# Narrow attention: project all heads once, stack rows by one-hot products, contract over 32 rows per head

## The chip, the cores and the metric

The kernel runs on one core of a Trainium2 chip. The metric is the device time of one execution in microseconds (us), lower is better. The profile is one profiled execution on the same core.

## The reference

A stack of four gated blocks works on x of shape (4, 256, 128), that is 1024 tokens of width 128, with a context of the same shape. Each block adds an attention and then a feed-forward layer to the residual. Two of the four attentions are "narrow": 16 heads of width 8. Only these are touched.

```python
# block 0
Q = (query @ Wq.T).reshape(B, T_q, 16, 8)      # query = layernorm(x)
K = (context @ Wk.T).reshape(B, T_c, 16, 8)
V = (context @ Wv.T).reshape(B, T_c, 16, 8)
attn = softmax(einsum('bqhd,bkhd->bhqk', Q, K) / sqrt(8))
out = einsum('bhqk,bkhd->bqhd', attn, V).reshape(B, T_q, D) @ Wo.T
# block 2: the same without any weights: Q = layernorm(x), K = V = context
x = x + tanh(g) * out
```

## The kernel before

Everything stays in SBUF. The narrow attention is `small_pe`, `small_act`, `small_dve`, called with c=0 for block 0 and c=1 for block 2. Heads go in NG = 4 groups of GH = 4; tokens go in two halves of 512 (two batches each). One (group, half) is a slot, x in the code; there are eight slots in each attention, the first four in a hardware loop (`Fori`), the other four written out.

Precision: the products run in fp32r, so each fp32 operand is split into a high part and a low remainder. A head takes a block of 32 rows in the 128 partitions: 24 rows hold three copies of its 8 numbers (high with high, high with low, low with high in one contraction), and rows 24 and 25 carry minus the row maximum.

For each slot, in this kernel:

- `project` (L350) makes q or k of one group and half in three 128x512 products (`mm3`, L180 to L182) in bank 5, from weights in which the columns of each head stand three times. ACT's `high` (L456) copies the bank as the high part, DVE's `stack` (L511) builds the stacked rows from both.
- `masked_keys` (L518, DVE) makes four copies of the stacked keys, each with only one head's 32 rows left. So every product of scores contracts over all 128 rows, though only 32 are non-zero.
- `maxima` (L359, PE) makes the scores with queries as rows, in eight steps of two 256-column products, in turn in banks 6 and 7; `largest` (L524, DVE) takes the row maxima of each step. Step n waits for the reduction of step n-2. This is done for slot x+1 during slot x.
- `minus` (L533, L534) splits the negated maxima, `maxima_back` (L367) transposes them, `queries` (L538) adds them to the stacked queries.
- `scores` (L374) makes transposed scores in four steps of four products; ACT takes the exponential of each step (L471, 128x1024). `values` (L384) multiplies with the values and a column of ones, with the four heads in the four 32-column groups of the output, in four steps. ACT copies the sums (L474), `sums_back` (L392) transposes them, `normalise` (L546, L547) divides.

Each engine works through a queue written out by hand. That of PE in one slot: scores 0, maxima 0 and 1, scores 1, maxima 2 and 3, values 0, scores 2, three products of `project`, maxima 4, values 1, maxima 5, scores 3, maxima 6, values 2, maxima 7, values 3, `sums_back`, `maxima_back`, and `project` of the queries of x+3, which waits for `normalise`. Ahead of slot 0 stands an opening: four times projection, high part and stacked rows, each waiting for the one before (one bank, one tile); masked keys; eight maxima steps; transposes.

Of the kernel before, what the change touches and what calls it, by code (L numbers as in the profile page):

```python
# [51 lines left out]
for _name, _width in (  # L52
    ("ident", P), ("spread", 2 * P), ("den_ones", 5 * BLK), ("lo_q", 1), ("lo_k", 1), ("one_rows", 1), ("head", GH),
    ("inv_n", 2 * NT), ("iota", E), ("gates", 8), ("nbias", 1), ("alpha", 1), ("rb2", E), ("ebias", E),
    ("rb1", 1), ("gamma", E), ("beta", E), ("b1", 4 * E), ("b2", E), ("quant_bias", P),
    ("ln_l_w", 1), ("ln_l_b", 1), ("ln_c_w", 1), ("ln_c_b", 1), ("bo", P),
    ("centroids", E), ("gate_w", E), ("router_w2", E), ("b_experts", P),
    ("W_Q", P), ("W_K", P), ("W_inv", P), ("router_w1", P), ("W_O", P), ("wv0", P), ("wo0", P),
    ("quant_w", P), ("lora_a", P), ("lora_b", P), ("sel_e", E * P),
):  # L60
    SMALL[_name] = (N_SMALL, _width)
    N_SMALL += _width
# [59 lines left out]
def build(nc, x, ctx_tok, ctx_t, mask, small, wa0, wf0, wb1, wf1, wa2, wb3, wf3, out):  # L122
    stack = ExitStack()
    with stack:  # L124
# [32 lines left out]
        RB1, RA2, CAP = 0, NQ * W_B, NQ * W_B + NG * W_A  # L157
# [27 lines left out]
        ld = {n: sem("loaded_" + n) for n in ("x", "ctx_t", "ctx_tok", "small", "mask", "a0", "f0", "b1", "f1", "a2", "b3", "f3")}  # L185
# [124 lines left out]
        A = signals("a", NG, w=2, q=4, hi=4, y=4, km=8, v=2, mx=16, red=16, m2=2, mt=2, yf=2, s=8, p=8, pv=8,  # L310
# [3 lines left out]
        a_y, a_yf, a_ky = wr[:, 0:1024], wr[:, 1024:2048], wr[:, 2048:3072]  # L314
        a_km = [wr[:, 3072 + 1024 * j:4096 + 1024 * j] for j in range(GH)]
        a_hi = wr[:, 7168:8192]
        a_wh, a_wl = wr[:, 8192:8448], wr[:, 8448:8704]
        a_vall = wf[:, 0:1024]
        a_vg = wf[:, 1024:2048].rearrange("p (t j c) -> p t j c", t=NT, j=GH)
        a_p = [wf[:, 2048 + 1024 * k:3072 + 1024 * k] for k in range(2)]  # L320
        a_m2 = wf[:, 4096:5120].rearrange("p (t j c) -> p t j c", t=NT, j=GH)
# [7 lines left out]
        def small_passes(eng, slot):  # L329


            with eng.Fori(0, NG - 2) as i:
                slot(i, 0, True, True, True)
                slot(i, 1, True, True, True)
            slot(NG - 2, 0, True, True, True)
            slot(NG - 2, 1, False, True, True)
            slot(NG - 1, 0, False, False, True)
            slot(NG - 1, 1, False, False, False)

        def small_pe(pe, c, m):  # L340
            def at(i, name, k):
                pe.wait_ge(A[name].sem, A[name].at(c, i, k))

            def project(i, x, k):
                h = x % 2
                at(i, "w", 2 * (x // 2) + 2)
                if k:
                    at(i, "y", 2 * x + 1)
                src = (half(ch, h), half(cl, h)) if k else (half(xh, h), half(xl, h))
                mm3(bank(5), (a_wh[:, k * P:(k + 1) * P], a_wl[:, k * P:(k + 1) * P]), src).then_inc(A["q"].sem, 1)  # L350

            def maxima(i, x, n):
                t, j0 = 4 * (x % 2) + n // 2, 2 * (n % 2)
                if n == 0:
                    at(i, "km", 4 * x + 4)
                if n >= 2:
                    at(i, "red", 8 * x + n - 1)
                for j in range(j0, j0 + 2):
                    last = nc.tensor.matmul(ps[:, 6 + n % 2, (j % 2) * S:(j % 2 + 1) * S],  # L359
                                            a_y[:, t * P:(t + 1) * P], a_km[j][:, (t // 2) * S:(t // 2 + 1) * S],  # L360
                                            start=True, stop=True)
                last.then_inc(A["mx"].sem, 1)

            def maxima_back(i, x):
                at(i, "m2", x + 1)
# [5 lines left out]
            def scores(x, u):  # L371
                b, kb = 2 * (x % 2) + u // 2, u % 2
                for j in range(GH):
                    last = nc.tensor.matmul(ps[:, 2 * (u % 2) + j // 2, (j % 2) * S:(j % 2 + 1) * S],  # L374
                                            a_km[j][:, b * S + kb * P:b * S + (kb + 1) * P],
                                            a_yf[:, b * S:(b + 1) * S], start=True, stop=True)
                last.then_inc(A["s"].sem, 1)

            def values(i, x, u):
                if u == 0:  # L380
                    at(i, "v", x + 1)
                at(i, "p", 4 * x + u + 1)
                for j in range(GH):
                    last = nc.tensor.matmul(ps[BLK * j:BLK * (j + 1), 4, (u // 2) * S:(u // 2 + 1) * S],  # L384
                                            a_vg[:, 4 * (x % 2) + u, j, :], a_p[u % 2][:, j * S:(j + 1) * S],
                                            start=u % 2 == 0, stop=u % 2 == 1)
                last.then_inc(A["pv"].sem, 1)

            def sums_back(i, x):
                at(i, "raw", x + 1)  # L390
# [5 lines left out]
            def slot(i, x, asking, projecting, maxing):  # L396
                def more(*tiles):
                    for n in tiles if maxing else ():
                        maxima(i, x + 1, n)

                at(i, "yf", x + 1)
# [12 lines left out]
                scores(x, 3)  # L414
                more(6)
                values(i, x, 2)
                more(7)
                values(i, x, 3)
                if projecting:
                    at(i, "y", 2 * (x + 2) + 2)  # L420
                sums_back(i, x)
                if maxing:
                    maxima_back(i, x + 1)
                if asking:
                    at(i, "att", x + 1)
                    project(i, x + 3, 0)

            for x in range(2):
                pe.wait_ge(s_xs, 2 * splits(m) + x + 1)
                if x:  # L430
                    at(0, "y", 2)
                project(0, x, 0)
                project(0, x, 1)
            for n in range(8):
                maxima(0, 0, n)
            maxima_back(0, 0)
            at(0, "y", 4)
            project(0, 2, 0)
            small_passes(pe, slot)

        def small_act(act, c):
# [7 lines left out]
            def at(i, name, k):  # L449
                act.wait_ge(A[name].sem, A[name].at(c, i, k))  # L450

            def high(i, x, k, used=True):
                at(i, "q", 2 * x + k + 1)
                if used:
                    at(i, "y", 2 * (x - 1) + k + 1)
                nc.scalar.activation(half(a_hi, k), bank(5), ACT.Copy).then_inc(A["hi"].sem, 1)  # L456

            def value_tiles(i, x):
                t = slice(4 * (x % 2), 4 * (x % 2) + 4)
                nc.scalar.activation(a_vg[:, t, :, 0:DH8],  # L460
                                     vsrc[:, t, bass.ds((i + x // 2) * BLK, BLK)].rearrange("p t (j d) -> p t j d", j=GH),
                                     ACT.Copy).then_inc(A["v"].sem, 1)

            def slot(i, x, asking, projecting, maxing):
                for u in range(4):
                    if projecting and u == 3:
                        high(i, x + 2, 1)
                    at(i, "s", 4 * x + u + 1)
                    if u >= 2:
                        at(i, "pv", 4 * x + u - 1)  # L470
                    nc.scalar.activation(a_p[u % 2], bank(2 * (u % 2), 2), ACT.Exp,  # L471
                                         scale=float(1.0 / np.sqrt(np.float32(DH8)))).then_inc(A["p"].sem, 1)
                at(i, "pv", 4 * x + 4)
                nc.scalar.activation(half(a_raw, x % 2), bank(4), ACT.Copy).then_inc(A["raw"].sem, 1)  # L474
                if projecting:
                    value_tiles(i, x + 2)
                if asking:
                    high(i, x + 3, 0)

            act.wait_ge(s_ainit, c + 1)  # L480
            for x in range(2):
                value_tiles(0, x)
            for x in range(2):
                for k in range(2):
                    high(0, x, k, used=x == 1)
            high(0, 2, 0)
            small_passes(act, slot)
# [7 lines left out]
        def small_weights(dve, c, i, raw, r0, loaded=None):  # L495

            if loaded is not None:
                dve.wait_ge(loaded, 16)
            wqk = raw[:, bass.ds(i * W_A + r0, 2 * P)]
            nc.vector.tensor_copy(a_wh, wqk).then_inc(A["w"].sem, 1)  # L500
            dve.wait_ge(A["w"].sem, A["w"].at(c, i, 1))
            nc.vector.tensor_tensor(a_wl, wqk, a_wh.bitcast(F32), ALU.subtract).then_inc(A["w"].sem, 1)

        def small_dve(dve, order, c, raw, r0, before_last=None):

            def at(i, name, k):
                dve.wait_ge(A[name].sem, A[name].at(c, i, k))

            def stack(i, x, k):
# [1524 lines left out]
```

## Time and profile before

| | |
|---|---|
| median of 3 runs | 985.93 us (984.32 to 990.7) |
| the profiled execution | 984.13 us, its span 982.3 us |
| busy, share of the span | PE 83%, DVE 70%, ACT 45%, POOL 20% |
| mean granted TensorE clock | 0.917 |

The span runs from the first to the last instruction; 1.8 us lie around it. PE is TensorE's matmuls, PEld its weight loads, DVE is VectorE, ACT ScalarE, POOL GpSimd. "L374" is line 374 of the kernel. A granted clock of 1.00 is 2.4 GHz, one of 0.50 is 1.2 GHz.

### The profile page before, as it was taken

To read this page: it belongs to the slowest core of one execution; us is meant where nothing else is said; L and a number is where in the kernel's file an instruction comes from. 1 tells how busy PE (TensorE), PEld (TensorE's weight loads), DVE (VectorE), ACT (ScalarE), POOL (GpSimd) and SP (SyncE) were. 2 spreads that over 40 slices of the span, in tenths; PEclk is the share of its full clock that TensorE was granted. 3 is DMA by queue.
4 is the path that set the end of the run, shared out by engine and by line. 5 is a ranking of instruction groups with operands and counts; after the bars stand their busy time and mean duration, and the time that the engine had idled before them with its cause. 6 is when DMAs were issued, how large, how long until landed. Compare 5 with 4: busy or idle time off the path is not lost. (4 is left out here: it accounts for less than half of the span.)

```text
span 982.3 us, 14218 instructions
## 1 busy us (share of the span) xinstructions
PE 810.8 (83%) x4970; PEld 578.9 (59%) x4970; DVE 686.0 (70%) x1279; ACT 444.2 (45%) x663; POOL 193.1 (20%) x152
## 2 busy tenths in 40 slices
PE   2688878968999878999748886479989858999996
PEld 1455546645666666777526554346566546777774
DVE  4688856656656655788767887756665676788785
ACT  2245443225545402999614444045545205555553
POOL 1000010003436411222300000213543410111112
PEclk9599999989999985999958999679999968999998
DMA  8000000040110100000200060000112000000000
GB/s 359 0 2 0 1 1 1 1 171 1 45 45 1 44 1 1 1 0 0 86 0 1 0 273 1 1 1 2 44 45 44 1 0 1 0 0 0 1 0 23
DMA packets 3079, 29.43 MB, mean 30 GB/s; under 512 B 496, under 2 KB 592, under 8 KB 1488
## 3 DMA queue, kind: packets, MB, share of 16 engines
q1 hardware_dynamic: 3024, 28.70, 8.4%
q8 instruction: 34, 0.56, 0.2%
q14 instruction: 21, 0.17, 0.1%
HBM read 28.07 MB, written 0.62 MB: 29 GB/s over the span
## 5 line engine op out<-in xcount | busy, mean ns | idle before, releaser
L180 PE MATMUL banks<-normed_t_high,work_split 128*128 128x512 f32 x264 | 120.3, 456 | 31.1 <-DVE work_split L892 10.9
L856 POOL TENSOR_TENSOR work<-work 128x512 f32<-128x512 f32 x64 | 85.6, 1338 | 160.9 <-PE banks L718 119.4
L182 PE MATMUL banks<-normed_t_high,work_split 128*128 128x512 f32 x264 | 108.5, 411 | 0.0
L181 PE MATMUL banks<-normed_t_low,work_split 128*128 128x512 f32 x264 | 108.5, 411 | 0.0
L524 DVE TENSOR_REDUCE work<-banks 128x2 f32<-128x512 f32 x128 | 84.9, 687 | 26.5 <-PE banks L359 26.1
L241 POOL TENSOR_TENSOR ln_rstd<-ln_var_eps,minus_half 128x8 f32<-128x8 f32 x10 | 17.9, 1789 | 366.0 <-DVE ln_var_eps L225 366.0
L471 ACT ACTIVATE work<-banks 128x1024 f32<-128x1024 f32 x64 | 65.3, 1024 | 47.2 <-PE banks L374 47.1
L180 PEld LDWEIGHTS banks<-normed_t_high,work_split 128*128 128x128 f32 x264 | 52.1, 197 | 54.1 <-issue 16.1
L1565 ACT ACTIVATE work<-banks 128x512 f32<-128x512 f32 x68 | 40.6, 598 | 73.2 <-PE banks L182 73.1
L1676 DVE TENSOR_TENSOR work<-work,banks 128x512 f32<-128x512 f32 x68 | 46.6, 686 | 38.1 <-ACT work L1565 37.6
L699 PE MATMUL banks<-work 128*64 128x256 f32 x512 | 69.5, 392 | 3.9 <-ACT work L823 3.9
L359 PE MATMUL banks<-work_split 128*128 128x256 f32 x256 | 60.4, 336 | 13.2 <-DVE work L524 10.1
L180 PE MATMUL banks<-work_split 128*128 128x512 f32 x148 | 64.2, 434 | 5.9 <-DVE work_split L1639 4.4
L1424 DVE TENSOR_TENSOR work_split<-work,work_split 128x512 fp32r<-128x512 f32 x64 | 51.1, 799 | 22.0 <-ACT work_split L1351 21.7
L359 PEld LDWEIGHTS banks<-work_split 128*128 128x128 f32 x256 | 42.5, 208 | 36.8 <-DVE work L524 25.7
L687 PEld LDWEIGHTS banks<-work_split 64*128 64x128 f32 x768 | 49.8, 187 | 24.1 <-issue 13.3
L687 PE MATMUL banks<-work_split 64*128 64x256 f32 x768 | 62.4, 296 | 0.0
L914 DVE SCALAR_TENSOR_TENSOR work<-banks,score_floor,raw_b 128x1024 f32<-128x1024 f32 x32 | 40.8, 1276 | 30.3 <-PE banks L687 30.3
L918 DVE TENSOR_SCALAR work<-banks 128x1024 f32<-128x1024 f32 x32 | 38.9, 1219 | 31.6 <-PE banks L687 31.5
L182 PEld LDWEIGHTS banks<-normed_t_high,work_split 128*128 128x128 f32 x264 | 52.2, 198 | 12.8
L181 PEld LDWEIGHTS banks<-normed_t_low,work_split 128*128 128x128 f32 x264 | 52.4, 198 | 12.4 <-issue 3.4
L182 PE MATMUL banks<-work_split 128*128 128x512 f32 x148 | 59.3, 401 | 0.0
(256 smaller groups left out, 1728.4 us busy)
## 6 DMA issues: line engine op xcount, KB each, us to landing
raw_b<-in_wf SPq DMA_DIRECT2D x1, 6528.0 KB, 19.0
raw_a<-in_wf SPq DMA_DIRECT2D x1, 4096.0 KB, 12.4
raw_b<-reciprocal_rows SPq DMA_DIRECT2D x6, 512.0 KB, 5.6
raw_a<-reciprocal_rows SPq DMA_DIRECT2D x6, 512.0 KB, 5.7
raw_a<-in_wf SPq DMA_DIRECT2D x1, 2048.0 KB, 13.2
raw_b<-in_wb SPq DMA_DIRECT2D x1, 2048.0 KB, 17.5
raw_a<-in_wb SPq DMA_DIRECT2D x1, 2048.0 KB, 7.9
small_operands<-in_small SPq DMA_DIRECT2D x1, 1687.0 KB, 7.2
```

The costliest lines, as they stand in the source:

```text
L180: nc.tensor.matmul(o, w[0], m[0], start=start, stop=False)
L181: nc.tensor.matmul(o, w[0], m[1], start=False, stop=False)
L182: return nc.tensor.matmul(o, w[1], m[0], start=False, stop=stop)
L359: last = nc.tensor.matmul(ps[:, 6 + n % 2, (j % 2) * S:(j % 2 + 1) * S], a_y[:, t * P:(t + 1) * P], a_km[j][:, (t // 2) * S:(t // 2 + 1) * S],
L471: nc.scalar.activation(a_p[u % 2], bank(2 * (u % 2), 2), ACT.Exp, scale=float(1.0 / np.sqrt(np.float32(DH8)))).then_inc(A["p"].sem, 1)
L524: nc.vector.tensor_reduce(a_nm[:, t, j0:j0 + 2], bank(6 + n % 2).rearrange("p (j k) -> p j k", j=2), AX.X, ALU.max, negate=True).then_inc( ...
L687: last = nc.tensor.matmul(ps[:, 2 * (g % 2) + h, kb * S:(kb + 1) * S], w_k[kt][rows, keys], w_q[qt][rows, b * S:(b + 1) * S], start=n == 0 ...
L699: last = nc.tensor.matmul(ps[DH * h:DH * (h + 1), 4, (b % 2) * S:(b % 2 + 1) * S], w_v[:, 2 * b + kb, (2 * p + h) * DH:(2 * p + h + 1) * D ...
L856: nc.gpsimd.tensor_tensor(w_ps[g % 2].rearrange("p (h q) -> p h q", h=2), v[:, :, 0, :], v[:, :, 1, :], ALU.add).then_inc(W["ps"].sem, 1)
L914: ins = nc.vector.scalar_tensor_tensor(out=v, in0=s, scalar=w_floor, op0=ALU.max, op1=ALU.min, in1=cap[:, g % 4, :, :].rearrange("p k q -> ...
L1424: nc.vector.tensor_tensor(g_a[n % 4][1], g_af[n % 4], g_a[n % 4][0].bitcast(F32), ALU.subtract)\
L1676: nc.vector.tensor_tensor(k_af[n % 2], k_sg[n % 2], bank(2 + n % 2), ALU.mult).then_inc(K["a"].sem, 1)
```

## The change

1. **Projection.** All 16 heads are projected at once (128 columns, no triple columns), q and k, two halves: four `mm3` into banks 2 to 5. ACT takes the high parts, DVE the low ones, once (`small_project_*`). Attention 1 has no projection; it takes the split tokens and context as they are.
2. **Stacked rows.** For each slot and for q and k, `rows` makes the 128 stacked rows by two 128x512 products with one-hot selectors (one for high, one for low), and ACT copies the bank (`stacked`; for keys with the bias `one_rows`). DVE's `stack`, `masked_keys` and `small_weights` per group are gone.
3. **32-row products.** `maxima` and `scores` read only the 32 rows of their head, on both sides.
4. **Order.** `values` goes in two steps of eight products, with four tiles for the exponentials instead of two; scores of one step are now both key blocks of two heads; maxima 0 of the next slot stands ahead of the wait for the queries.
5. **No hardware loop**: eight slots written out, so that waits are on constants.
6. **Opening.** PE also runs 33 products of the identity with itself (`stream`), whose output nobody reads: three behind each of the four `rows`, two behind each of the eight maxima steps, three before and two behind `maxima_back`.
7. **Around it.** The weights load is a quarter as large, two loads of 0.5 MB bring the selectors in place of one of 0.5 MB; ACT copies the selectors to fp32r ahead of both attentions; DVE's `split_ctx` moves from behind the first layer norm into its wait for GpSimd.

```diff
-        A = signals("a", NG, w=2, q=4, hi=4, y=4, km=8, v=2, mx=16, red=16, m2=2, mt=2, yf=2, s=8, p=8, pv=8,
+        A = signals("a", NG, yp=4, y=4, v=2, mx=16, red=16, m2=2, mt=2, yf=2, s=8, p=8, pv=4,
                     raw=2, rt=2, att=2)
...
+        def small_project_pe(pe):
+            pe.wait_ge(s_aw, 2)
+            for n in range(4):
+                h, k = n // 2, n % 2
...
+                mm3(bank(2 + n), [w[:, k * P:(k + 1) * P] for w in a_w], src).then_inc(s_aq, 1)
...
+            def rows(x, k):
...
+                elif k:
+                    at("y", 2 * x + 1)
+                else:
+                    at("att", x - 2)
+                hi, lo = (((xh, xl), (a_kh, a_kl)), ((xh, xl), (ch, cl)))[c][k]
+                nc.tensor.matmul(bank(a_bank(x, k)), a_selector(k, g, 0), half(hi, h), start=True, stop=False)
+                nc.tensor.matmul(bank(a_bank(x, k)), a_selector(k, g, 1), half(lo, h), start=False, stop=True)\
+                    .then_inc(A["yp"].sem, 1)
...
+                    last = nc.tensor.matmul(ps[:, 7 - n % 2, e * S:(e + 1) * S], a_y[a_rows(j), t * P:(t + 1) * P],
+                                            half(a_ky, x % 4)[a_rows(j), pair * S:(pair + 1) * S],
+                                            start=True, stop=True)
...
+                for kb in range(2):
+                    for j in range(2 * (u % 2), 2 * (u % 2) + 2):
+                        last = nc.tensor.matmul(ps[:, j, kb * S:(kb + 1) * S],
+                                                half(a_ky, x % 4)[a_rows(j), b * S + kb * P:b * S + (kb + 1) * P],
+                                                half(a_yf, x % 2)[a_rows(j), b * S:(b + 1) * S],
+                                                start=True, stop=True)
...
+                more(0)
+                at("yf", x + 1)
                 scores(x, 0)
-                more(0, 1)
+                more(1)
                 scores(x, 1)
                 more(2)
+                scores(x, 2)
                 more(3)
-                values(i, x, 0)
-                scores(x, 2)
-                if projecting:
-                    project(i, x + 2, 1)
+                if x + 2 < STEPS:
+                    rows(x + 2, 0)
                 more(4)
-                values(i, x, 1)
+                values(x, 0)
+                scores(x, 3)
                 more(5)
-                scores(x, 3)
-                more(6)
-                values(i, x, 2)
-                more(7)
-                values(i, x, 3)
-                if projecting:
-                    at(i, "y", 2 * (x + 2) + 2)
-                sums_back(i, x)
-                if maxing:
-                    maxima_back(i, x + 1)
-                if asking:
-                    at(i, "att", x + 1)
-                    project(i, x + 3, 0)
+                if x + 2 < STEPS:
+                    rows(x + 2, 1)
+                more(6, 7)
+                values(x, 1)
+                if x + 2 < STEPS:
+                    at("y", 2 * (x + 2) + 2)
+                sums_back(x)
+                if x + 1 < STEPS:
+                    maxima_back(x + 1)
...
+            pe.wait_ge(s_sel, 2 * c + 2)
             for x in range(2):
+                rows(x, 0)
+                stream(3, 6)
+                rows(x, 1)
+                stream(3, 6)
             for n in range(8):
+                maxima(0, n)
+                stream(2)
+            stream(3)
+            maxima_back(0)
+            stream(2)
+            for x in range(STEPS):
+                slot(x)
...
             def slot(x):
                 for u in range(4):
+                    if u == 3 and x + 2 < STEPS:
+                        stacked(x + 2, 0)
+                    at("s", 4 * x + u + 1)
+                    if x:
+                        at("pv", 2 * (x - 1) + u // 2 + 1)
+                    nc.scalar.activation(a_p[u], bank(2 * (u % 2), 2), ACT.Exp,
                                          scale=float(1.0 / np.sqrt(np.float32(DH8)))).then_inc(A["p"].sem, 1)
+                if x + 2 < STEPS:
+                    stacked(x + 2, 1)
+                at("pv", 2 * x + 2)
                 nc.scalar.activation(half(a_raw, x % 2), bank(4), ACT.Copy).then_inc(A["raw"].sem, 1)
...
-                if projecting:
-                    at(i, "s", 4 * x + 4)
-                    masked_keys(i, x + 2, (0, 1))
-                normalise(i, x)
-                if maxing:
-                    queries(i, x + 1)
-                if projecting:
-                    masked_keys(i, x + 2, (2, 3))
+                more(0, 1, 2, 3, 4, 5, 6, 7)
+                if x + 1 < STEPS:
+                    minus(x + 1)
+                normalise(x)
+                if x + 1 < STEPS:
+                    queries(x + 1)
```

## Rows read from the trace of the kernel before

**Rows 1.** The page: granted clock of the span in 40 slices, in tenths.
```profile
PEclk9599999989999985999958999679999968999998
```
**Rows 2.** Busy time of each engine by stretch, with granted clock (PEclk).
```profile
25.00:30.00 5.00, 2.92 (x6) 1.97 (x7) 3.07 (x6) 0.60 (x1) 0.00 (x0) 0.50 0.00 0
498.00:501.00 3.00, 1.65 (x3) 0.83 (x3) 1.32 (x3) 1.30 (x4) 0.00 (x0) 0.50 0.00 0
43.00:131.00 88.00, 74.67 (x586) 49.67 (x585) 69.71 (x136) 44.51 (x58) 0.00 (x0) 0.99 0.00 1
...
368.00:376.00 8.00, 7.86 (x37) 7.46 (x36) 5.25 (x16) 0.95 (x2) 3.77 (x4) 0.50 0.01 3
250.00:275.00 25.00, 23.05 (x207) 14.50 (x205) 19.21 (x20) 15.30 (x21) 12.48 (x9) 1.00 0.19 45
```
**Rows 3.** The timeline, PE alone: first product and first scores of each narrow attention.
```profile
20.45 0.50 PE L180 MATMUL banks<-normed_t_high,work_split 128*128 128x512 f32 x1 [1.11 <-ACT work L1782]
...
43.04 1.05 PE L374 MATMUL banks<-work_split 128*128 128x256 f32 x4
...
498.06 0.79 PE L180 MATMUL banks<-normed_t_high,work_split 128*128 128x512 f32 x1 [0.39 <-DVE normed_t_low L270]
...
521.92 1.05 PE L374 MATMUL banks<-work_split 128*128 128x256 f32 x4
```
**Rows 4.** The timeline, PE alone: the last transposes of the sums, both attentions.
```profile
131.15 0.65 PE L392 MATMUL banks<-small_operands,work 128*128 128x128 f32 x4 [0.72 <-ACT work L474]
...
610.00 0.66 PE L392 MATMUL banks<-small_operands,work 128*128 128x128 f32 x4 [0.72 <-ACT work L474]
```
**Rows 5.** The timeline of all engines over one slot of the loop.
```profile
67.11 0.63 PE L374 MATMUL banks<-work_split 128*128 128x256 f32 x4
...
68.29 1.98 DVE L524 TENSOR_REDUCE work<-banks 128x2 f32<-128x512 f32 x3 [0.59 <-PE banks L359]
...
69.00 1.02 ACT L471 ACTIVATE work<-banks 128x1024 f32<-128x1024 f32 x1 [0.18 <-PE banks L374]
...
72.23 0.64 PE L384 MATMUL banks<-work 128*32 128x256 f32 x8
...
72.80 0.51 PE L359 MATMUL banks<-work_split 128*128 128x256 f32 x2
...
73.62 0.40 PE L359 MATMUL banks<-work_split 128*128 128x256 f32 x2
...
75.65 0.60 ACT L474 ACTIVATE work<-banks 128x512 f32<-128x512 f32 x1 [0.81 <-PE banks L384]
...
76.39 0.63 PE L392 MATMUL banks<-small_operands,work 128*128 128x128 f32 x4 [0.81 <-ACT work L474]
...
77.73 0.68 DVE L538 TENSOR_TENSOR work_split<-banks,work_split 128x512 fp32r<-128x512 f32 x1
...
78.68 0.64 PE L374 MATMUL banks<-work_split 128*128 128x256 f32 x4
```
**Rows 6.** The timeline, PE alone: a slot written out, start and next start.
```profile
102.22 0.64 PE L374 MATMUL banks<-work_split 128*128 128x256 f32 x4
...
113.49 0.73 PE L374 MATMUL banks<-work_split 128*128 128x256 f32 x4 [0.84 <-DVE work_split L538]
```
**Rows 7.** The timeline, PE: the wide attention's 64-row products, two row blocks in turn.
```profile
233.81 0.98 PE L687 MATMUL banks<-work_split 64*128 64x256 f32 x12
...
234.72 0.50 PE L180 MATMUL banks<-normed_t_high,work_split 128*128 128x512 f32 x1
```
**Rows 8.** The timeline: eight fp32 products of 128 columns (two records each).
```profile
134.38 2.05 PE L285 MATMUL banks<-small_operands,work 128*128 128x128 f32 x16 [0.74 <-ACT work L612]
```
**Rows 9.** Groups by line, whole span: the DVE work that goes.
```profile
L518 DVE TENSOR_SCALAR work_split<-work_split,small_operands 128x512 fp32r<-128x512 f32 x64 | 31.6, 541 | 0.1
L511 DVE SCALAR_TENSOR_TENSOR work_split<-work_split,small_operands,banks 128x512 fp32r<-128x512 f32 x32 | 23.8, 743 | 13.2 <-ACT work_split L456 13.2
```
**Rows 10.** DMA issues (KB, us from issue to landing) and the step that moves, on DVE.
```profile
raw_a<-in_wa SPq DMA_DIRECT2D x1, 512.0 KB, 8.8
...
19.01 1.22 DVE L1703 TENSOR_TENSOR context_t_low<-sublayer_out_t,context_t_high 128x1024 fp32r<-128x1024 f32 x1
```

More of the change, by code:

```diff
@@ L326, in build @@
         a_att_t = wf[:, 1024:2048]
[L329 to L338, printed above, removed]
-        def small_pe(pe, c, m):
[L341 to L353, printed above, removed]
-                if n == 0:
[L355 to L360, printed above, removed]
@@ new lines, in small_project_act, with small_project_dve @@
+        def small_project_act(act):
+            for n in range(4):
+                act.wait_ge(s_aq, n + 1)
+                nc.scalar.activation(half((xh, a_kh)[n % 2], n // 2), bank(2 + n), ACT.Copy).then_inc(s_ah, 1)
+        def small_project_dve(dve):
+            for n in range(4):
+                dve.wait_ge(s_ah, n + 1)
+                hi, lo = ((xh, xl), (a_kh, a_kl))[n % 2]
+                nc.vector.tensor_tensor(half(lo, n // 2), bank(2 + n), half(hi, n // 2).bitcast(F32), ALU.subtract)\
+                    .then_inc(s_al, 1)
@@ L441, in small_act, with small_selectors_act @@
+            for x in range(STEPS):
+                slot(x)
+        def small_selectors_act(act, c):
+            if c == 0:
+                act.wait_ge(ld["sel"], 32)
+            for k in range(2):
+                nc.scalar.activation(a_sel[:, 1024 * k:1024 * (k + 1)], raw_b[:, RSEL[k]:RSEL[k] + 1024], ACT.Copy)\
+                    .then_inc(s_sel, 1)
         def small_act(act, c):
@@ L447, in small_act, with at @@
             vsrc = vsrc.rearrange("p (t d) -> p t d", t=NT)
[L449 to L458, printed above, removed]
+            def at(name, k):
+                act.wait_ge(A[name].sem, A[name].at(c, 0, k))
@@ new lines, in stacked @@
+            def stacked(x, k):
+                at("yp", 2 * x + k + 1)
+                src = bank(a_bank(x, k))
+                if k:
+                    if x >= 4:
+                        at("s", 4 * (x - 4) + 4)
+                    ins = nc.scalar.activation(half(a_ky, x % 4), src, ACT.Identity, bias=col("one_rows"))
+                else:
+                    if x >= 2:
+                        at("yf", x - 1)
+                    ins = nc.scalar.activation(half(a_y, x % 2), src, ACT.Copy)
+                ins.then_inc(A["y"].sem, 1)
@@ L477, in slot @@
-                if asking:
-                    high(i, x + 3, 0)
+                if x + 2 < STEPS:
+                    value_tiles(x + 2)
+            for x in range(2):
+                stacked(x, 0)
+                stacked(x, 1)
             act.wait_ge(s_ainit, c + 1)
             for x in range(2):
[L482 to L487, printed above, removed]
+                value_tiles(x)
@@ L489, in small_pool @@
+            for x in range(STEPS):
+                slot(x)
         def small_pool(pool, c):
@@ L582, in small_dve @@
+                more(0, 1, 2, 3, 4, 5, 6, 7)
[4 more added lines that the diff above has]
+                    queries(x + 1)
             for n in range(8):
-                largest(0, 0, n)
+                largest(0, n)
             dve.wait_ge(s_ainit, c + 1)
-            minus(0, 0)
-            queries(0, 0)
-            with dve.Fori(0, NG - 2) as i:
-                order.loop(i, 4)
-                slot(i, 0, True, True, True)
-                slot(i, 1, True, True, True)
@@ L591, in small_dve @@
-            order.end(NG - 2)
-            slot(NG - 2, 0, True, True, True)
-            slot(NG - 2, 1, False, True, True)
-            slot(NG - 1, 0, False, False, True)
-            if before_last is not None:
-                before_last()
-            slot(NG - 1, 1, False, False, False)
+            minus(0)
+            queries(0)
+            for x in range(STEPS):
+                if x == STEPS - 1 and before_last is not None:
+                    before_last()
+                slot(x)
```

246 lines of the change are left out of this document (117 added, 129 removed).

## The prediction, as put on record

> **What bounds the kernel now.** I read first the granted clock of the page, then busy time by stretch, then the timeline of one slot of the narrow attention, and last its two openings. The page shows a clock near full nearly everywhere, with dips at a few slices [rows 1]. The two narrow attentions take from 20.45 to 131.15 us and from 498.06 to 610.00 us [rows 3, 4]: 110.7 + 111.9 = 223 us of the 982. Each has two parts: an opening of 22.6 us (20.45 to 43.04) or 23.9 us (498.06 to 521.92), and eight slots of 88.1 us in both cases (43.04 to 131.15, 521.92 to 610.00).
>
> In the slots the clock is 0.99; PE is busy 74.7 of 88 us and DVE 69.7, ACT only half [rows 2]. So neither is simply full: the order and the round trips bound it. In one slot [rows 5] the scores begin at 67.11 and those of the next slot at 78.68: 11.57 us. DVE's first reduction begins at 68.29, that is 1.2 us after the scores, since maxima 0 stands behind scores 0 and behind the masked keys. The tail is serial: sums copied at 75.65, transposes at 76.39, queries at 77.73, scores at 78.68. In the openings the clock is 0.50 [rows 2]: PE waits after every product for ACT's copy and DVE's stacking before it may use bank 5 again, and DVE makes masked keys twice before the first reduction.
>
> **Prices.** A record's end is modelled some 0.17 us behind the last column, so I price PE by what is left or by the next start. Four 256-column products: 0.63 - 0.17 = 0.46 us, 0.115 each; a step of maxima (two) 0.40 - 0.17 = 0.23; four products of `values` 72.80 - 72.23 = 0.57, of which about 0.10 is the change of shape, as the first pair after it shows (0.51 against 0.40); four transposes 0.63 - 0.17 = 0.46 [rows 5]. Exponential 1.02, reductions 0.65 apart (1.98 for three), copy of a bank 0.60, `queries` 0.68 [rows 5]. An engine picks up another's result 0.05 us after its end (69.00 + 1.02 against the first possible 70.07 for `values` in this slot; I take 0.05 throughout).
>
> 32-row products do not occur. The nearest row is the 64-row products of the wide attention, which alternate between two row blocks and banks: twelve in 234.72 - 233.81 = 0.91 us, 0.076 each [rows 7]. Scores of the new kernel also alternate between two blocks, so I take 0.076 for them (0.30 a step), with 0.115 (no overlap) as the upper bound and 0.03 (four at once) as the lower. Maxima 0 to 7 stay in one block within a step; I take 0.115 and bound it by 0.20, as if the weight load of the second could no longer hide. For each change between 32-row, 128-row and 32-column products I take 0.10, bounds 0 and 0.20.
>
> The Trainium skill, "TensorE: Matmul & The Clock Gate", section on what overlaps in packed products, says that a weight load runs beside a product only if it goes to another row block (or to the spare weight buffer). Here 128-row products on the same rows follow each other at 0.115 us, 256 columns at 2.4 GHz being 0.107, so their loads are hidden. If the strict half of the rule held for 32 rows, the step of maxima would be at its upper bound; that is the rival "exposed loads" below. "TensorEngine Tiling (Array Packing)", key properties, says that a change of tiling mode drains the engine. The 0.10 in rows 5 is such a cost as measured; a larger one is the upper bound above.
>
> **One new slot.** Start at the scores, time 0. DVE no longer does stacks and masks: 2 x 0.74 and 4 x 0.49 (31.6 / 64) go, 3.4 us a slot with projections [rows 9], and eight reductions, `minus`, `normalise`, `queries` are left, about 6.9. ACT keeps its load: four exponentials, two stacked copies for two high parts, sums, values. The walk:
> - Scores 0 are out at 0.30 + 0.17, the exponential ends at 1.54. PE has done maxima 1, scores 1 and maxima 2 by then.
> - Scores 2 wait for this exponential (same banks): 1.59. Now PE runs through: scores 2 0.30, maxima 3 0.23, `rows` with its two changes of shape 0.46 + 0.20, maxima 4 0.23, values of eight products with the change 1.04, scores 3 0.40, maxima 5 0.23, `rows` 0.66, maxima 6 and 7 0.46, `values` 1.04, and 0.17 to its end. Sum 5.42, and 0.07 in small waits for reductions: 7.08. The last exponential, fed by scores 3 at 4.06, ends at 5.70 and is in time.
> - Copy of the sums 0.05 + 0.60, pick-up 0.05: transposes at 7.78. `maxima_back` follows 0.47 later; 0.64 until it can be read, 0.08 to DVE, `queries` 0.68, pick-up 0.05: 9.70.
> - DVE: reductions run from -0.13 (maxima 0 came early) to 7.13 with waits, `minus` ends 7.57, ahead of 8.25. So DVE has 0.7 us to spare in that place and PE's queue decides.
>
> So 9.70 us. The same walk with the old queue and prices gives 11.0 and 11.9 in turn; the trace has 11.57 and 11.27 (102.22 to 113.49, no loop) [rows 5, 6], so the recipe is good to some 3%, and waits on constants are worth 0.3 us at most. Seven slots, the last 0.5 shorter for want of projections, and the last until its transposes (7.3) make 67.4 + 7.3 = 74.7, against 88.1: 13.4 us for each attention. By bounds: without any overlap of scores 78.0 (10.17 a slot), changes at 0.20 in addition 81; best case 70.
>
> **Openings.** Attention 0: `split_ctx` (two steps, the larger 1.22 [rows 10]) now fills DVE's wait for GpSimd and outlasts it by under 1 us, which the layer norm gives back only in part, since its tiles then run clear of GpSimd's clearing; I count 0.4 us later. The selectors stand behind a quarter-sized weights load; the old one landed 8.8 us after its issue [rows 10] at about 10.9 us, so they should be there by 12.5 and copied by 14.5, ahead of ACT's first norm copy at 16; nothing for it. PE starts projecting about 1 us before the old 20.45, since it no longer waits for the values copy: 19.6. Four `mm3`, three products of 512 columns at 0.23 each, 0.70, with copies and lows under them: 22.4. Each `rows` is 0.43 with three identity products of 0.235 ((2.05 - 0.17) / 8 [rows 8]): 1.14, four times 4.6: 26.9. Maxima: 0.23, two identities 0.47, changes 0.20, so 0.90 a step, 7.2: 34.1. Here the identities, not DVE's 0.65, set the pace. Then three identities (or the end of `minus`) until 34.95, transposes 0.64 and 0.08 to DVE, `queries` 0.68, pick-up 0.05: 2.3. Scores at 36.4 against 43.04: 6.6 us less. All this at full clock: PE has work without gaps from 19.6 on, where the old PE, at 0.50, was busy 2.9 of 5 us [rows 2].
>
> Attention 1 starts at 498.06 at half clock. How long it stays there under steady work no row of mine tells; I charge 4 us, between the bounds of none and all. These do 1.7 of the four `rows` (2.36 each at half clock), the rest take 2.6: 504.7; then 7.2 + 2.3: 514.2 against 521.92, 7.7 less. Bounds: if the clock stays at 0.50 throughout, 4 x 2.36 + 8 x 1.6 + 3.5 = 25.6, 1.7 us more than before.
>
> **Sum.** 2 x 13.4 + 6.6 + 7.7 = 41 us from 984.1: 943 for the profiled execution. That stood 1.8 under the median; against the median 945. DMA: 0.5 MB more ahead of the feed-forward weights, some 1.5 us at loads needed a hundred us later, hidden. The second selector copy, 2 us of ACT, lies in the layer norm ahead of attention 1, where ACT has nothing to do.
>
> **Rivals.**
> - *Exposed loads.* Maxima pairs cost 0.20 a product and scores nothing less than 0.115: the walk gives 10.96 a slot and 83.5 for eight. Gain 2 x 4.6 + 13 = 22 us, 963 by the median. For it: identical row blocks within each maxima step. Against: the 0.115 of the 128-row products. 12%.
> - *The change does less in the slots.* Slot time is set by the tail and round trips, not by what goes, and stays at 11.3, as a slot written out has now: only the openings gain, 14 us: 971. For it: DVE's masks lie partly beside the serial tail. Against: the old first reduction 1.2 us after the scores, and PE's queue that is a microsecond shorter. 6%.
> - *The clock falls in the slots* (slower). A 32-row product uses a quarter of the rows. That busy time is no warrant is seen at 368 to 376: PE busy 7.86 of 8 us with one-column products, clock 0.50. Against: with 64-row products 1.00 at 250 to 275 [rows 2]. At half clock products and changes double; the walk gives 13.6 a slot, 103.5 for eight: 2 x 15.4 more, less 14 in the openings: plus 17, 1003. It decides when the clock is low in over half of the slots' time. 8%.
> - Clock late only in the openings: 5 to 9 us lost, inside the range.
>
> **Chances and range.** The forecast's own case 74%: 932 (best overlap, no cost for changes, 2 x 18 + 15) to 962 (no overlap, dear changes, 2 x 7 + 10). The range must reach the exposed loads and no further: 932 to 966. Outside are the two last rivals and the clock. A measurement of this kernel tells 1%, 10 us, from nothing. Faster by more: 89%; within 1%: 4%; slower by more: 7%.
>
> **What would show it.** Slots 9.7 us apart in PE's timeline; scores steps of 0.30 and maxima steps of 0.23; reductions beginning beside the scores; L518 and L511 gone and nothing in their place on DVE; clock 1.00 from 20 us to 125 and from about 502 us; first scores near 36 us and 514 us (less the 13 to 20 us by which the second attention comes earlier). I am wrong if the scores products are no faster than 0.115, if PE's steps have gaps of 0.3 and more at changes of shape, if the clock is low in the slots, or if another wait (the exponential ring, the stacked copies on ACT) ends last.

## The result

The changed kernel takes 1005.35 us (median of 4 runs), the kernel before 985.22: the ratio is 1.020, with a 95% interval from 1.015 to 1.024. It is slower by 20 us, where 945 us was forecast; whether by more than 2% the interval leaves open. The profiled execution has a span of 1002.8 us against 982.3.

The page of the changed kernel, granted clock, against [rows 1]:

```profile
PEclk9865658989999985999976556579999978999998
```

Two troughs have come, slices 3 to 6 and 22 to 26 (each 25 us): both narrow attentions. By stretch, against 0.99 in the slots of before [rows 2] (the columns are those of rows 2; the last three numbers are clock, DMA share, GB/s):

```profile
20.00:38.00 18.00, 18.00 (x108) 14.87 (x107) 8.66 (x15) 6.22 (x11) 0.38 (x1) 1.00 0.23 97
41.00:116.00 75.00, 66.89 (x434) 36.76 (x434) 37.92 (x72) 34.07 (x47) 0.00 (x0) 0.61 0.00 1
515.00:590.00 75.00, 69.06 (x436) 41.35 (x438) 39.30 (x71) 30.06 (x41) 0.00 (x0) 0.64 0.00 1
```

The opening runs at 1.00, the slots at 0.61 and 0.64, though PE is busy 67 and 69 of 75 us there. DVE's work did shrink as intended: 38 us in 75, against 70 in 88 before. PE's busy share is no help here: products at half clock are simply longer.

The timeline of PE shows where slots begin (first scores of each; 5 of 16 rows), where attention 1 starts, and where both end:

```profile
38.70 0.52 PE L418 MATMUL banks<-work_split 32*128 32x256 f32 x8
...
90.21 0.81 PE L418 MATMUL banks<-work_split 32*128 32x256 f32 x8
...
104.76 0.81 PE L418 MATMUL banks<-work_split 32*128 32x256 f32 x8
...
138.91 1.12 PE L439 MATMUL banks<-small_operands,work 128*128 128x128 f32 x4 [0.72 <-ACT work L541]
...
509.37 0.77 PE L389 MATMUL banks<-normed_t_high,work_split 128*128 128x512 f32 x1 [0.48 <-DVE normed_t_low L271]
...
526.23 0.52 PE L418 MATMUL banks<-work_split 32*128 32x256 f32 x8
...
537.25 0.52 PE L418 MATMUL banks<-work_split 32*128 32x256 f32 x8 [0.41 <-DVE work_split L590]
...
627.25 1.12 PE L439 MATMUL banks<-small_operands,work 128*128 128x128 f32 x4 [0.72 <-ACT work L541]
```

From one slot's first scores to the next it takes between 11.0 us (526.23 to 537.25, clock 0.85) and 14.55 (90.21 to 104.76, clock 0.50), against 10.7 to 12.2 in the kernel before. The sum over the run, in us, from the first product and the first and last rows of each attention [rows 3, 4]:

| | before | changed | difference |
|---|---|---|---|
| start to first scores, attention 0 | 43.04 | 38.70 | -4.3 |
| eight slots, attention 0 | 88.1 | 100.2 | +12.1 |
| from there to attention 1 | 366.9 | 370.5 | +3.6 |
| opening, attention 1 | 23.9 | 16.9 | -7.0 |
| eight slots, attention 1 | 88.1 | 101.0 | +12.9 |
| from there to the end | 372.3 | 375.6 | +3.3 |

The stages behind each attention also lose some 3 us: they begin at a lower clock. The first 10 us behind the last transposes of attention 0, in the changed kernel and then in the one before:

```profile
139.00:149.00 10.00, 9.00 (x39) 7.65 (x40) 4.56 (x16) 1.85 (x4) 0.00 (x0) 0.59 0.01 2
```

```profile
131.40:141.40 10.00, 8.10 (x46) 5.41 (x44) 6.05 (x28) 4.13 (x8) 1.52 (x1) 1.00 0.00 0
```

Behind attention 1 it is 0.50 (627.5 to 637.5) against 0.76 (610.2 to 620.2). The whole is 20.6; the spans differ by 20.5.

### The profile page after: what moved, and what is told of

Its sections match the earlier page's. It is cut to its first block and busy times, and to the rows that moved or that the text cites. A ratio compares the mean times of both kernels' runs of the same rounds, so it can differ in the third digit from the quotient of the medians.

```text
span 1002.8 us, 14014 instructions
## 1 busy us (share of the span) xinstructions
PE 851.2 (85%) x5082; PEld 591.5 (59%) x5082; DVE 636.1 (63%) x1173; ACT 451.6 (45%) x671; POOL 192.6 (19%) x152
## 5 line engine op out<-in xcount | busy, mean ns | idle before, releaser
L181 PE MATMUL banks<-normed_t_high,work_split 128*128 128x512 f32 x250 | 112.4, 450 | 22.6 <-DVE work_split L919 10.9
L182 PE MATMUL banks<-normed_t_low,work_split 128*128 128x512 f32 x250 | 101.7, 407 | 0.0
L183 PE MATMUL banks<-normed_t_high,work_split 128*128 128x512 f32 x250 | 101.6, 406 | 0.0
L726 PE MATMUL banks<-work 128*64 128x256 f32 x512 | 72.1, 404 | 4.1 <-ACT work L850 4.1
L181 PEld LDWEIGHTS banks<-normed_t_high,work_split 128*128 128x128 f32 x250 | 49.0, 196 | 41.6 <-DVE work_split L919 12.1
L400 PE MATMUL banks<-work_split 32*128 32x256 f32 x256 | 70.2, 412 | 1.1 <-DVE work L576 0.8
L181 PE MATMUL banks<-work_split 128*128 128x512 f32 x148 | 64.4, 435 | 6.0 <-DVE work_split L1666 4.4
L536 ACT ACTIVATE work<-banks 128x1024 f32<-128x1024 f32 x32 | 31.0, 1021 | 63.0 <-PE banks L418 63.0
L182 PE MATMUL banks<-work_split 128*128 128x512 f32 x148 | 59.1, 399 | 0.0
L400 PEld LDWEIGHTS banks<-work_split 32*128 32x128 f32 x256 | 45.8, 252 | 22.4 <-DVE work L576 15.8
L183 PE MATMUL banks<-work_split 128*128 128x512 f32 x148 | 58.9, 398 | 0.0
L182 PEld LDWEIGHTS banks<-normed_t_low,work_split 128*128 128x128 f32 x250 | 49.3, 197 | 12.4 <-issue 3.4
## 6 DMA issues: line engine op xcount, KB each, us to landing
raw_a<-in_wf SPq DMA_DIRECT2D x1, 4096.0 KB, 12.2
```

The lines of the kernel that those rows point to most:

```text
L181: nc.tensor.matmul(o, w[0], m[0], start=start, stop=False)
L182: nc.tensor.matmul(o, w[0], m[1], start=False, stop=False)
L183: return nc.tensor.matmul(o, w[1], m[0], start=False, stop=stop)
L400: last = nc.tensor.matmul(ps[:, 7 - n % 2, e * S:(e + 1) * S], a_y[a_rows(j), t * P:(t + 1) * P], half(a_ky, x % 4)[a_rows(j), pair * S:(p ...
L726: last = nc.tensor.matmul(ps[DH * h:DH * (h + 1), 4, (b % 2) * S:(b % 2 + 1) * S], w_v[:, 2 * b + kb, (2 * p + h) * DH:(2 * p + h + 1) * D ...
```

## Why the clock falls: four runs

Two theories. A: the products that fill only 32 of the 128 rows let the clock fall. B: the new order does it, with its waits and its fewer columns. The 32-row products differ from 128-row ones in two ways at once, in the rows that they fill and in that they overlap in time; both belong to A. All experiments start from the changed kernel unless said otherwise; their row-dependent edits touch `maxima` and `scores` alone.

**128 rows in each product.** The output is that of four summed heads. `c_rows` takes the place of `a_rows` in both operands of `maxima` and `scores`; the diff shows one of these lines.

```diff
+        def c_rows(j):
+            return slice(0, P)
...
-                                                half(a_yf, x % 2)[a_rows(j), b * S:(b + 1) * S],
+                                                half(a_yf, x % 2)[c_rows(j), b * S:(b + 1) * S],
```

> The changed kernel with every maxima and scores product contracting over all 128 rows in place of its head's 32, so that four heads are summed (the output is then not the reference's); order, waits and count of products are as in the changed kernel. Theory A (the clock falls since the products fill only 32 of the 128 rows): clock 1.00 from 20 us to the end of each narrow attention, slots of 9.9 to 10.4 us (no overlap of scores, but no changes of shape either), 945 us, 935 to 960. Theory B (the clock falls for the new order with its waits and fewer columns, whatever the rows): clock near 0.6 in the slots and 1000 us, as now.

Measured 954.89 us, ratio 0.969 (0.967 to 0.970). The timeline of PE, first scores of three slots in a row:

```profile
67.08 0.74 PE L421 MATMUL banks<-work_split 128*128 128x256 f32 x4 [0.59 <-DVE work_split L593]
...
77.53 0.74 PE L421 MATMUL banks<-work_split 128*128 128x256 f32 x4 [0.59 <-DVE work_split L593]
...
87.98 0.75 PE L421 MATMUL banks<-work_split 128*128 128x256 f32 x4 [0.59 <-DVE work_split L593]
```

10.45 us a slot, and the stretch:

```profile
41.00:116.00 75.00, 60.24 (x533) 43.71 (x532) 47.41 (x91) 40.19 (x54) 0.00 (x0) 1.00 0.00 1
```

Same order, same waits, same count of products: clock 1.00. Theory B is out. This version also has no overlap of products and no changes between 32 and 128 rows, so it does not say which of these goes with the clock. PE is busy 60 of 75 us here, less than the 67 of the changed kernel.

**64 rows.** Two heads summed.

```diff
+        def c_rows(j):
+            return slice(64 * (j // 2), 64 * (j // 2 + 1))
```

> The same with 64 rows a product, two heads summed (output not the reference's). Theory A: the 64-row products of the wide attention ran at 1.00 beside other work, so the clock is full for all or most of the slots; 945 to 975 us. Theory B: 1000 us.

Measured 966.65, 979.38, 987.82 and 1011.79 us, at mean clocks of 0.918, 0.905, 0.886 and 0.863: the time follows the clock. In the profiled run (979.38) attention 0 kept slots of 10.38 us but for the last, clock 0.95, and attention 1 lost the clock halfway (four slots of 10.4, then 14.9, 16.1 and 11.6):

```profile
41.00:116.00 75.00, 61.35 (x536) 39.29 (x535) 48.19 (x93) 40.00 (x54) 0.00 (x0) 0.95 0.00 1
515.00:590.00 75.00, 66.11 (x476) 41.91 (x469) 41.48 (x79) 34.85 (x48) 0.00 (x0) 0.77 0.00 1
```

So the same instructions at 64 rows hold or lose the clock from one stretch to the next, and from one run to the next. The row of 64-row products in the wide attention that I leaned on [rows 2] was no assurance.

**The kernel before with 32-row maxima only.** Order, masked keys and scores stay; a step is one head and two token tiles, so that two row blocks never write one bank unordered. DVE's reduction reads in the new order (not in the diff).

```diff
-                for j in range(j0, j0 + 2):
+                for e in range(2):
+                    t = 4 * (x % 2) + 2 * pair + e
...
-                                            a_y[:, t * P:(t + 1) * P], a_km[j][:, (t // 2) * S:(t // 2 + 1) * S],
+                                            a_y[M_ROWS(j), t * P:(t + 1) * P],
+                                            a_km[j][M_ROWS(j), (t // 2) * S:(t // 2 + 1) * S],
```

> The kernel before, with only the maxima products changed: each reads the 32 rows of its head of the masked keys and of the queries, and a step is one head and two token tiles. All else, masked keys too, stays. Theory A: about half of the slot's scores columns are 32-row, so the clock falls in part of the slots; clock of 43 to 131 us between 0.6 and 0.9, 990 to 1010 us. Theory B: the order is the old one, so the clock stays at 0.99 and the time is 985, or up to 3 us lower or higher for the changes of shape.

Measured 1015.26, 1015.47 and 1015.57 us at a mean clock of 0.887, and 994.9 us at 0.916. The kernel before took 984.39 to 990.69 us beside them, at 0.909 to 0.917. In the profiled run, the one of 1015.26 us, the clock of this stretch is 0.82, against 0.97 in the kernel before:

```profile
41.00:116.00 75.00, 66.99 (x412) 42.34 (x410) 53.65 (x106) 31.44 (x43) 0.00 (x0) 0.82 0.00 1
```

So one part of the change, alone in the old order, can bring the loss; this agrees with theory A. It is weaker evidence than the 128-row version: the run of 994.9 us is some 10 us slower than runs of the kernel before at the same mean clock, so these are not the clock's, and what they are stays open.

**Five identity products a slot in PE's gaps.**

```diff
                 values(x, 1)
+                stream(3, 0)
...
                 more(0)
+                stream(2, 0)
                 at("yf", x + 1)
```

> The changed kernel with five more products of the identity with itself in each slot, where PE waits: three behind the second step of values, two behind maxima 0 of the next slot. Both theories: if steady full-row work there is enough to hold the clock, slots of about 10 us and 950 us; if the products between still pull it down, slots of 13 us and 1000 to 1010. Theory A gives it a third, since the fill is 1.2 us of a slot of 10; Theory B more, since the fill removes the two longest gaps.

Measured 984.59 us (975.98 to 990.67, 10 runs), ratio 0.998 (0.995 to 1.001). Clock 0.81 and 0.89. Slots that kept the full clock took 9.85 us, those that lost it up to 14.0 (58.28 to 72.31). The full-clock slots price the walk; the timeline of all engines, a part of one:

```profile
48.43 0.52 PE L418 MATMUL banks<-work_split 32*128 32x256 f32 x8
...
48.97 1.94 ACT L538 ACTIVATE work<-banks 128x1024 f32<-128x1024 f32 x2 [2.55 <-PE banks L418]
...
50.05 0.38 PE L418 MATMUL banks<-work_split 32*128 32x256 f32 x2 [0.68 <-ACT work L538]
...
50.49 0.50 PE L389 MATMUL banks<-normed_t_high,work_split 128*128 128x512 f32 x1
50.80 1.03 ACT L538 ACTIVATE raw_a<-banks 128x1024 f32<-128x1024 f32 x1
50.83 0.40 PE L390 MATMUL banks<-normed_t_low,work_split 128*128 128x512 f32 x1
51.15 0.50 PE L400 MATMUL banks<-work_split 32*128 32x256 f32 x2
51.58 1.07 PE L430 MATMUL banks<-work 128*32 128x256 f32 x16
...
58.28 0.52 PE L418 MATMUL banks<-work_split 32*128 32x256 f32 x8
```

Scores 2 wait for the first exponential, 1.62 us after scores 0 (walk: 1.59). Scores 2 and maxima 3, six products, take 50.49 - 50.05 = 0.44 us, 0.073 each: row blocks do overlap, at the price taken from the 64-row row (0.076, [rows 7]). `rows` with its changes of shape is 51.15 - 50.49 = 0.66, as priced. A slot is 58.28 - 48.43 = 9.85 with the fill.

This run also bears on the two halves of theory A. Overlap takes array time away: the slot has 32 products in `scores` and `maxima`, so at most 32 x (0.115 - 0.073) = 1.3 us, by estimate. The fill gives 5 x 0.235 = 1.2 us of it back, and the clock still falls. That speaks for the rows themselves. It is no proof, and 32-row products kept from overlapping were not tried.

## What holds the clock, and a faster version: six runs

**Masked copies back, 128 rows, full computation.** Two of the four copies of a slot are made by ACT, two by DVE. `maxima` and `scores` read these copies over all rows (not in the diff). To fit them in, the projected keys take the place of the split context, which DVE splits again in the last slot.

```diff
+            def masked(x):                      # on ACT; DVE has the same for heads 0 and 1
+                at("y", 2 * x + 2)
+                if x >= 2:
+                    at("s", 4 * (x - 2) + 4)
+                for j in (2, 3):
+                    nc.scalar.activation(half(a_km[j], x % 2), half(a_ky, x % 2).bitcast(F32), ACT.Copy,
+                                         scale=col("head", j, 1)).then_inc(A["ka"].sem, 1)
```

> The changed kernel with masked key copies back and all maxima and scores products over 128 rows, of which 96 are zero for each head (full computation). ACT makes two of the four copies of a slot behind the value tiles, where it waits for PE; DVE makes the other two between minus and normalise. Theory A (rows streamed count, zeros or not): clock 1.00 in the slots, slots of 10.45 us as in the run with summed heads, or up to 10.8 for DVE's two copies; 950 to 962 us. Theory B2 (the clock answers to non-zero work in the rows, that is to the data): the summed heads had all rows non-zero and these have a quarter, so it falls as in the changed kernel, 1000 us.

Measured 955.28 us, ratio 0.970 (0.966 to 0.973); slots of 10.45. This beats both kernels, 3% under the one before. The data theory falls: 96 of the 128 rows of each key operand are zero, and the clock is 1.00. The kernel before had told as much, with masked keys at 0.99 [rows 2]. The stretch, and from the timeline DVE's and ACT's copies, which lie beside PE's tail:

```profile
41.00:116.00 75.00, 61.09 (x533) 43.87 (x533) 54.52 (x105) 47.54 (x66) 0.00 (x0) 1.00 0.01 1
```

```profile
85.42 0.88 DVE L598 TENSOR_SCALAR work_split<-work_split,small_operands 128x512 fp32r<-128x512 f32 x2
...
86.08 1.32 ACT L532 ACTIVATE work_split<-work_split,small_operands 128x512 fp32r<-128x512 f32 x2
86.13 0.63 PE L442 MATMUL banks<-small_operands,work 128*128 128x128 f32 x4 [0.81 <-ACT work L553]
```

**128-row maxima, 32-row scores** (masked copies as above; column ranges left out of the diff).

```diff
-    half(a_km[j], x % 2)[:, ...], half(a_yf, x % 2)[:, ...]      # scores
+    half(a_km[j], x % 2)[a_rows(j), ...], half(a_yf, x % 2)[a_rows(j), ...]
```

> The same, but scores read only their head's 32 rows; maxima stay at 128. Theory A: half of the slot's scores columns are full again, so the clock is between the two; the kernel before with 32 rows in maxima alone had 0.83 in the slots. Here the same share gives 0.8 to 1.0 and 955 to 985 us. If half is enough, overlapped scores save 0.15 us a step and the time is 945 to 955, under the 128-row version.

Measured 963.12 us, ratio 0.977 (0.974 to 0.981). Slots are shorter, 10.25, at clock 1.00 from 36 to 106 us, yet the whole is longer: in the profiled run the last slot of each attention, which has no `maxima` and no `rows`, and the stage behind ran at half clock (0.50 from 112 to 120 us and from 577 to 588). The same eight fp32 products behind attention 0, here and in the 128-row version, in two fences:

```profile
121.23 3.78 PE L286 MATMUL banks<-small_operands,work 128*128 128x128 f32 x16 [0.69 <-ACT work L665]
```

```profile
119.21 2.05 PE L286 MATMUL banks<-small_operands,work 128*128 128x128 f32 x16 [0.74 <-ACT work L665]
```

The profiled spans differ by 4.2 us (957.4, 953.2), the medians by 8; where the rest lies I did not find.

**No identity products in the openings** (128-row masked version).

```diff
             def stream(n, k=4):
...
-                for _ in range(n):
-                    nc.tensor.matmul(ps[:, k, 0:P], ident, ident, start=True, stop=True)
+                pass
```

> As the 128-row masked version, with the products of the identity in the openings left out. Theory C (they hold the clock up and are worth their time): clock 0.50 in the openings and the first slot, first scores 1 to 4 us later in each attention, so plus 2 to 10 us. Rival D (the shorter opening with fewer waits needs no fill): each opening is up to 3 us shorter, as the maxima steps then take 0.65 us in place of 1.07; minus 3 to 8 us.

Measured 957.77 us, 0.971 (0.967 to 0.974): the interval covers that of the version with them. Up to the first scores of attention 0 both effects are there and cancel: 35.73 without and 35.76 with them, though the clock from 20 to 38 us is 0.74 against 1.00. Slot 0 then takes 11.43 instead of 10.46, and in the profiled runs the last transposes of attention 1 come at 580.99 against 577.99. So the identity products may be worth some 3 us, but not the openings' gain: first scores at 35.73 stand against 43.04 in the kernel before. How that gain divides between projecting once and `rows` without DVE was not taken apart.

**Eleven and eight identity products a slot**, 32-row products, full computation. The diff is that of eleven; the version with eight leaves out `stream(3)`.

```diff
                 more(0)
+                stream(4, 0)
                 at("yf", x + 1)
...
                 more(2)
+                stream(3)
                 scores(x, 2)
...
                 values(x, 1)
+                stream(4, 0)
```

> The changed kernel with eleven products of the identity in each slot (four behind the last values, four behind maxima 0 of the next slot, three before scores 2), 2.6 us of PE a slot. Theory A: the clock is above the 0.80 to 0.85 that five gave, 0.9 to 1.0; slots of 10.5 to 11 us and 955 to 975 us. If the 32-row stretches by themselves pull the clock down, it stays near 0.85 and the time at 985 or above.

> The changed kernel with eight products of the identity a slot, four behind the last values and four behind maxima 0, none before scores 2. Five held the clock only in part (0.81 and 0.89 in the slots) with 9.85 us in the slots that had it, eleven held it whole with 10.40. Theory A: at eight it is whole or nearly so, and the fill of the queue before the copy of the sums costs at most what its gap hides: slots 9.85 to 10.2, 948 to 962 us. If the clock still breaks in some slots, 960 to 980.

Eleven: 959.65 us, 0.972 (0.969 to 0.975). Eight: 966.31 us, 0.981 (0.980 to 0.983). Both have slots of 10.40 at clock 1.00, with all 32-row products and all their changes of shape in place, and more of these changes around the fill: so these changes are not what lets the clock fall. The three before scores 2 lie in the wait for the exponential and cost nothing; three more of the others cost 0.55 over 9.85. The profiled runs (960.33 and 962.11 us) differ by 1.8 us, and attention 0 shows where: with eight the clock falls in its last slot, and the last transposes of the sums come at 119.95 in place of 118.00. The same stretch, with eleven and then with eight:

```profile
112.00:120.00 8.00, 5.62 (x62) 3.79 (x61) 2.68 (x8) 3.77 (x5) 0.00 (x0) 1.00 0.01 2
```

```profile
112.00:120.00 8.00, 5.79 (x49) 3.61 (x50) 1.73 (x2) 3.99 (x5) 0.00 (x0) 0.71 0.01 2
```

The medians differ by 7 us; the rest is not in the profiled runs and stays open.

**Mixed version with five fills.** The two edits above together.

> The masked version with 128-row maxima and 32-row scores, and five products of the identity in the gaps of each slot. Without them the slots took 10.25 us, and the clock was 0.95 and 0.91, with 0.70 and 0.63 behind the attentions. Theory A: clock 1.00 in the slots, which stay at 10.25, and the stage behind each attention starts with it; 948 to 956 us, that is at or under the 128-row masked version.

Measured 963.81 us, 0.978 (0.977 to 0.980): a miss. The clock was 1.00 from 36 to 106 and from 498 to 568 us, as it had been without the fill, and the eight fp32 products behind attention 0 took 2.05 us again. But the last slots still lost the clock in part (0.66 from 112 to 120 us, 0.69 from 577 to 588), and the other slots went from 10.25 to 10.70: the fill is not covered by gaps there, and six slots twice at 0.45 cost 5.4 us.

## Why the prediction was wrong

The step that failed is the clock in the slots. The sum took it as full and counted 74.7 us for eight slots; measured are 100.2 and 101.0, at a clock of 0.61 and 0.64. These are 51.8 of the 61.6 us between forecast and profiled execution; openings (3.0) and following stages (6.9) are the rest. The prediction had this as a rival, "the clock falls in the slots", with 8% and 1003 us. It came true, by its own test too: a mean of 0.61 between the levels 1.00 and 0.50 is half clock for nearly four fifths of that stretch. What was wrong was the argument against it: 64-row products at clock 1.00 in another stage. Those stood between 128-row products. The run with 64 rows in this place loses the clock in part.

That 1003 came within 2 us of 1005 is in part luck. At half clock throughout a slot took 14.55, not 13.6, but the clock was not low throughout, so eight slots took less than the 103.5 of that walk; the openings gained less than its 14 us, and the 6.9 us of the following stages were not in it.

- *Prices and walk.* Right where the clock held: 9.85 with five fills against 9.70 forecast. With 128 rows it is 10.45 against 10.17 for no overlap, and that 10.17 still has changes of shape which this version lacks, so there the walk was short by more than the 0.28. Part of it is in the timeline: the last maxima step waits 0.29 us for a reduction of DVE, where the walk had 0.07 for all such waits.

```profile
73.32 0.30 PEld L403 LDWEIGHTS banks<-work_split 128*128 128x128 f32 x2 [0.29 <-DVE work L579]
```

- *Exposed loads.* Two maxima steps of the opening, timeline of PE, in the changed kernel and then in the 128-row masked version:

```profile
27.98 0.50 PE L400 MATMUL banks<-work_split 32*128 32x256 f32 x2
28.41 0.71 PE L475 MATMUL banks<-small_operands 128*128 128x128 f32 x4
29.06 0.50 PE L400 MATMUL banks<-work_split 32*128 32x256 f32 x2
```

```profile
27.07 0.48 PE L403 MATMUL banks<-work_split 128*128 128x256 f32 x2
27.39 0.60 PE L478 MATMUL banks<-small_operands 128*128 128x128 f32 x4
27.75 0.48 PE L403 MATMUL banks<-work_split 128*128 128x256 f32 x2
```

  From the pair to the identities it takes 0.43 against 0.32. Exposed loads at 0.20 a product would have added 0.17 and a change of shape on top; the 0.11 are less than the first alone. How they divide between load and change these rows do not tell. The Trainium skill, "TensorE: Matmul & The Clock Gate", Part 3, "The mechanism", lets a load run ahead of a product in flight if it goes to a row group without conflict or to the background weight buffer. A load on the same rows that is hidden, fully or nearly, agrees with the second.
- *Openings.* Forecast -6.6 and -7.7; -4.3 and -7.0 measured. The maxima step was mis-sized: 1.08 us (27.98 to 29.06) against 0.90 forecast and 0.68 with 128 rows, so the two changes of shape, with what is left of exposed loads, cost 0.40 there, not 0.20; the projections of attention 0 began at 20.16, not 19.6. In the slots `rows` with its two changes took 0.66, as priced.
- *Following stages.* Not in the sum at all: 3.6 and 3.3 us lost, from a clock that was low when they began.
- *Range.* 932 to 966 left out the clock. Its lower end does not follow from its terms (985.9 less 51 is 935), which changes nothing here. The versions that hold the clock in most slots, other kernels than the one forecast, lie at 954.9 to 966.3.

## What to carry to other kernels

A product that uses a quarter of the rows is not free of charge for using less: in this kernel the clock of all PE work around it fell to half for most of the time, and the work after it was slower too. Before narrowing products, look whether the engine's other work keeps full rows, and measure the new order once with full rows, heads summed: that tells the effect of the narrow products from that of the order in one run. Zero rows were as good as full ones for the clock, so a masked copy on a waiting engine can be worth more than the array time that it wastes.

## What the runs showed of the hardware

- With order, waits and columns equal, clock in the slots: 0.61 and 0.64 with 32 rows (attention 0 and 1, the stretches above), 0.95 and 0.77 with 64, 1.00 in both with 128 (41 to 116 and 498 to 568 us). Overlap and changes of shape go with the rows here; the changes are ruled out by the runs with fills, against the overlap speaks only an estimate.
- 128-row products with 96 zero rows in one operand keep 1.00 (masked version), as those with all rows filled do.
- PE busy 67 of 75 us at 0.61, and 60 of 75 at 1.00: busy share does not tell the clock.
- 32-row products in different row blocks and banks overlap: 0.073 us each for 256 columns (six in 0.44), against 0.115 for 128-row ones.
